# Four score blocks per exponential instead of two, and a layernorm that reads PSUM without a copy, in an eight-core transformer layer

## The chip, the cores and the metric

The kernel runs on the 8 cores of one Trainium2 chip, the same program on every core with other data. The metric is the device time of the slowest core in microseconds (us). Each core has a matrix engine (PE, with its weight loads shown apart as PEld), a vector engine (DVE), a scalar engine (ACT), GpSimd (POOL) and a queue engine (SP) that here only starts transfers. PE writes into PSUM, 2048 float32 columns in each of the two tensors `ps_a` and `ps_b2` of this kernel, cut into banks of 512 columns.

## The reference

Four sequences of 2048 tokens of width 2048 go through one attention layer and one gated MLP, each with a layernorm before and behind it:

```python
# attention: 16 query heads of 128, 4 key/value heads; causal, 1024 wide, plus the first 4 tokens
att = einsum('bkgqd,bkjd->bkgqj', q, k) / sqrt(128)
y   = softmax(where(mask, att, -inf)) @ v
# layer
x = x + layernorm(attention(layernorm(x)))            # _L0_attn_ref, Wq Wk Wv Wo
x = x + layernorm(ffn(layernorm(x)))                  # silu(h @ Wg.T) * (h @ Wu.T) @ Wd.T, 8192 wide
```

## The kernel before

Each core takes one half (1024 tokens) of one sequence as queries; keys and values cover up to 2048 tokens. Weights come in as float32 through two staging tiles (`stage`, L244) and are cast to bf16 on ACT or POOL. There is no scheduler: the Python code calls `em.task(engine, ...)`, each engine executes its tasks in the order of these calls, and the class `Em` works out from named tiles which semaphores a task waits for. A task waits only before its first instruction and signals only behind its last. So the order of the calls on each engine is the order of the work.

The stages, with times since the start of the span of the profiled execution:

- 0 to 367 us: layernorm of 16 token tiles, their transposes, and the k, v and q projections. The tile `xt` of 1 MB comes by a transfer that POOL issues (L354), K and V projections stand between (`kproj`, `vproj`).
- 367 to about 708 us: attention. A head is handled in two half-loops that run one head apart. `front_batch` (L436) makes scores: it multiplies one to two blocks of 128 keys with 512 queries into banks of `ps_a` (L448, 128x512 each), takes their exponential on ACT into `pt` in bf16 (L457) and multiplies by the mask on DVE (L476). The table `FRONT_B` gives the blocks of each batch; batches of even number use banks 0 and 1, those of odd number banks 2 and 3 (`base`, L440). `back_batch` (L487) handles the head before: four value matmuls and four matmuls with a column of ones (which sum the softmax) per batch of four blocks, by the table `BATCHES`, into `ps_b2`. `back_norm` (L521) belongs to the head before that: one matmul, then a copy, a logarithm and an exponential of 128x512 on ACT (L530, L532, L535), and a multiplication on DVE. The order within head `i` is: back batch 0 of head `i-1`, front batch 0, the norm of head `i-2`, front batch 1, back batch 1, front batches 2 and 3, and so on. There are 32 such heads: 16 over the first 512 queries (12 blocks of keys each, called the first half below), then 16 over the other 512 (13 blocks, the second half); between the halves another mask tile is loaded over the first.
- 708 to 862 us: output projection of 8 token tiles, layernorm, residual, second layernorm and transposes.
- 862 to 2200 us: the MLP in four quarters, PE after PE.
- 2200 to 2283 us, the last stage: for each of 8 token tiles, 16 float32 transposes (L769) bring the MLP's result from `out_fm` into PSUM, all of `ps_b2` for even tiles and all of `ps_a` for odd ones. ACT copies the tile to SBUF (L779), DVE takes its statistics (L785, L790). That is `e_stage1`. `e_stage2` makes the reciprocal deviation on ACT (L803, L806), the shift on DVE (L809), the normalised tile on ACT in place (L813), adds the residual on DVE (L819) and stores. The calls are `e_stage1(tb)`, then `e_stage2(tb - 1)` (L827 to L830).

Of the kernel before, what the change touches and what calls it, by code (L numbers as in the profile page):

```python
# [27 lines left out]
FRONT_B = [  # L28
    [(0, 2), (2, 2), (4, 2), (6, 2), (8, 2), (10, 2)],
    [(0, 2), (2, 2), (4, 2), (6, 2), (8, 2), (10, 2), (12, 1)],  # L30
]
# [95 lines left out]
def build_nc():  # L127
# [75 lines left out]
    pa = ps_a.ap()  # L203
# [145 lines left out]

    for idx, tb in enumerate(TB_ORDER):  # L350
# [3 lines left out]
        em.task("gpsimd",  # L354
                [lambda q, tb=tb, s=s: q.dma_start(out=xt[s].ap(),
                                                   in_=x_kv[tb * 128:(tb + 1) * 128, :])],
                writes=[f"xt{s}"], stream=f"xt{s}")
# [78 lines left out]
    def front_batch(qs, hh, bi):  # L436
        kl = KL[qs]
        kv = hh // 4
        st0, ln = FRONT_B[qs][bi]
        base = (bi % 2) * 2  # L440
        fns = []
        bkeys = []
        for j in range(ln):
            s_ = st0 + j
            kb = kl[s_]
            bkeys.append(PAK[base + j])
            fns.append(lambda t, kb=kb, kv=kv, dst=PA[base + j], qs=qs, hh=hh:
                       t.matmul(dst,  # L448
                                kf.ap()[:, kv * 2048 + kb * 128:kv * 2048 + (kb + 1) * 128],
                                qf.ap()[:, hh * 1024 + qs * 512:hh * 1024 + (qs + 1) * 512],  # L450
                                start=True, stop=True, skip_group_check=True))
# [5 lines left out]
                [lambda q, base=base, st0=st0, ln=ln: q.activation(  # L457
                    pt.ap()[:, st0 * 512:(st0 + ln) * 512],
                    pa[:, base * 512:(base + ln) * 512],
# [86 lines left out]
    for i, (qs, hh) in enumerate(HSEQ):  # L546
# [195 lines left out]
    def e_stage1(tb):  # L742
# [33 lines left out]
        war_o = [otkey + "ln"] + (["xo1"] if s == 1 else  # L776
                                  ["h2tok", "x2t_1", "x2p_1"])
# [16 lines left out]
    def e_stage2(tb):  # L794
# [6 lines left out]
        otkey = "outT" if s == 0 else "xo1"  # L801
        b6, b2_, rs, nm, _ = STT[par]
# [147 lines left out]
```

How the kernel before makes its waits and increments, by code:

```python
    def replay(self, eng_obj, eng_name, sems):  # L112
        for waits, fns, inc in self.items[eng_name]:
            for (s, v) in waits:
                eng_obj.wait_ge(sems[s], 16 * v if s in self.streams else v)
            last = None
            for fn in fns:
                last = fn(eng_obj)
            if inc is not None and last is not None:
                last.then_inc(sems[inc[0]], inc[1])
```

## Time and profile before

| | |
|---|---|
| median of 3 runs | 2284.46 us (2282.42 to 2285.09) |
| profiled execution | 2284.57 us; span of its slowest core, core 4: 2282.9 us |
| spans of the eight cores | 2269.5 to 2282.9 us, granted PE clock 0.969 to 0.972 on each |
| PE busy | 2025.4 us, 89% of the span |
| ACT busy | 955.6 us, 42% |
| DVE busy | 459.7 us, 20% |
| chain that ended last | PE 82%, ACT 9%, issue 4%, DVE 3%, DMA 2% |

Around the span lie 1.7 us of the profiled execution. A busy share is an average over stages of different kinds: what an edit is worth is read in its own stage, from which engine waits for which there. In the rows a matmul's end is modelled and neighbours overlap, so distances between starts are surer than lengths; a row with "x4" spans four instructions. A few matmul records are missing, so a row may say x1 where two instructions ran.

### The profile page before, as it was taken

Reading aid. Unit: us, or ns where it says so; the run is one execution under the profiler, and the core shown is the slowest. Engines: PE = TensorE matmul, PEld = TensorE weight load, DVE = VectorE, ACT = ScalarE, POOL = GpSimd, SP = SyncE. Lnnn points to the kernel's source line nnn. Section 1 sums busy time; section 2 is a strip of 40 time slices with the busy share of each in tenths; the row PEclk is TensorE's granted clock in tenths of the full one; section 3 lists DMA queues with packets and bytes.
Section 4 is the critical chain, followed back from the end, with each engine's and each line's share of the span. In section 5 each row is a group of like instructions: output and inputs, shape, how many; then the busy total and the mean of one; then the engine's idle time right before and its main releaser. Section 6 shows DMA issues by size and latency. Waiting matters only on the chain.

```text
span 2282.9 us, 24237 instructions; the slowest of 8 cores (2269.5 to 2282.9 us)
## 1 busy us (share of the span) xinstructions
PE 2025.4 (89%) x9241; PEld 897.6 (39%) x9424; DVE 459.7 (20%) x672; ACT 955.6 (42%) x1043; POOL 65.5 (3%) x87
## 2 busy tenths in 40 slices
PE   0677999998888878999999999999999999999971
PEld 0333443222223433444444444444444444444441
DVE  1122003553333450000110000110001110001134
ACT  3344346887774434333323333313333323333324
POOL 1100002400000000000000000000000000000000
PEclk9988999999999998999999999999999999999995
DMA  6321245501001334444643444534445534445515
GB/s 185 129 88 60 93 148 182 180 1 49 1 1 56 111 116 152 157 148 148 189 144 125 152 153 155 190 110 148 148 157 162 180 111 156 156 149 166 186 73 221
DMA packets 75570, 298.71 MB, mean 131 GB/s; under 512 B 8512, under 2 KB 8640, under 8 KB 69056
## 3 DMA queue, kind: packets, MB, share of 16 engines
q1 hardware_dynamic: 70848, 263.58, 35.8%
q0 software_dynamic: 4608, 33.56, 4.2%
q8 instruction: 77, 1.26, 0.2%
q14 instruction: 37, 0.30, 0.1%
HBM read 280.33 MB, written 16.78 MB: 130 GB/s over the span
## 4 chain that ended last, share of the span: by engine, by line
PE 82%; ACT 9%; issue 4%; DVE 3%; DMA 2%; ACTq 0%; DVEq 0%; SPq 0%; POOL 0%; POOLq 0%
PE ps_b L674 19%; PE ps_a L682 19%; PE ps_a L715 10%; PE ps_b L715 10%; PE ps_a L407 3%; PE ps_b L507 3%; PE ps_a L448 3%; ACT pt L457 3%; PE ps_b L498 3%; PE ps_a L590 3%; PE ps_b L590 2%; PE ps_a L312 2%; PE ps_a L327 2%; PE ps_b L407 2%; ACT h1t L375 1%
## 5 line engine op out<-in xcount | busy, mean ns | idle before, releaser
L253 ACT CAST wbf<-wst 128x1024 bf16<-128x1024 f32 x384 | 394.4, 1045 | 468.3 <-DMA wst<-wgu_pe 231.8
L674 PE MATMUL ps_b<-h2f,wbf 128*128 128x512 bf16 x2006 | 451.6, 380 | 6.5 <-ACT wbf L253 4.4
L682 PE MATMUL ps_a<-h2f,wbf 128*128 128x512 bf16 x2008 | 449.7, 379 | 2.1
L674 PEld LDWEIGHTS ps_b<-h2f,wbf 128*128 128x128 bf16 x2048 | 200.9, 98 | 247.3 <-issue 7.2
L682 PEld LDWEIGHTS ps_a<-h2f,wbf 128*128 128x128 bf16 x2048 | 200.4, 98 | 241.7
L694 DVE TENSOR_TENSOR a_sb<-silu_t,ps_a 128x1024 bf16<-128x1024 f32 x64 | 78.2, 1221 | 817.6 <-PE ps_a L682 578.4
L715 PE MATMUL ps_a<-a_sb,wbf 128*128 128x512 bf16 x1005 | 225.2, 379 | 6.9 <-DVE a_sb L694 5.9
L715 PE MATMUL ps_b<-a_sb,wbf 128*128 128x512 bf16 x1002 | 225.1, 379 | 1.2
L690 ACT ACTIVATE silu_t<-ps_b 128x1024 f32<-128x1024 f32 x64 | 65.6, 1025 | 380.4 <-PE ps_b L674 380.4
L457 ACT ACTIVATE pt<-ps_a 128x1024 bf16<-128x1024 f32 (+1 forms) x208 | 194.1, 987 | 69.6 <-PE ps_a L448 69.2
L476 DVE TENSOR_TENSOR pt<-pt,msk 128x1024 bf16<-128x1024 bf16 (+1 forms) x192 | 124.8, 662 | 292.2 <-ACT pt L457 283.0
L715 PEld LDWEIGHTS ps_a<-a_sb,wbf 128*128 128x128 bf16 x1024 | 99.9, 98 | 127.6 <-issue 7.8
L715 PEld LDWEIGHTS ps_b<-a_sb,wbf 128*128 128x128 bf16 x1024 | 100.2, 98 | 120.8
L448 PE MATMUL ps_a<-qf,kf 128*128 128x512 bf16 x387 | 113.7, 383 | 36.3 <-ACT pt L457 34.9
L383 PE MATMUL ps_b<-i,h1t 128*128 128x128 bf16 x256 | 23.2, 263 | 101.9 <-ACT h1t L375 101.9
L507 PE MATMUL ps_b<-pt,ones_bf 128*1 128x512 bf16 x400 | 105.2, 380 | 0.7
L498 PE MATMUL ps_b<-pt,vt 128*128 128x512 bf16 x388 | 102.6, 379 | 3.3 <-DVE pt L476 1.9
L407 PE MATMUL ps_a<-h1f,wqr 128*128 128x512 bf16 x344 | 76.5, 379 | 3.1 <-ACT wqr L253 2.7
L448 PEld LDWEIGHTS ps_a<-qf,kf 128*128 128x128 bf16 x400 | 26.6, 97 | 111.2 <-issue 103.2
L590 PE MATMUL ps_a<-wo_bf,yf 128*128 128x512 bf16 x249 | 57.6, 391 | 7.3 <-ACT h2f L636 4.6
L590 PE MATMUL ps_b<-wo_bf,yf 128*128 128x512 bf16 x252 | 57.3, 387 | 6.5 <-ACT h2f L636 6.3
L383 PEld LDWEIGHTS ps_b<-i,h1t 128*128 128x128 bf16 x256 | 20.0, 120 | 107.9 <-issue 107.9
(106 smaller groups left out, 1109.3 us busy)
## 6 DMA issues: line engine op xcount, KB each, us to landing
wst<-wgu_pe SPq DMA_DIRECT2D x256, 512.0 KB, 4.4
wst<-wd_pe SPq DMA_DIRECT2D x128, 512.0 KB, 4.5
xt<-x_kv POOLq DMA_DIRECT2D x16, 1024.0 KB, 5.2
wst<-wq_pe SPq DMA_DIRECT2D x32, 512.0 KB, 4.3
wst<-wo_t SPq DMA_DIRECT2D x32, 512.0 KB, 4.5
xo<-x_kv POOLq DMA_DIRECT2D x8, 1024.0 KB, 7.1
wst<-wk_pe SPq DMA_DIRECT2D x8, 512.0 KB, 4.7
wst<-wv_t SPq DMA_DIRECT2D x16, 256.0 KB, 3.9
```

The lines of the kernel that those rows point to most:

```text
L253: fn = [lambda g, d=dst_ap, sl=slot, n=n: g.copy(d, sl.ap()[:, 0:n])]
L407: fns.append(lambda t, r=r, ts=ts, c=c, bk=bk: t.matmul(bk, wqr[r].ap()[:, c * 128:(c + 1) * 128], h1f.ap()[:, c * 2048 + 1024 + ts * 512: ...
L448: t.matmul(dst, kf.ap()[:, kv * 2048 + kb * 128:kv * 2048 + (kb + 1) * 128], qf.ap()[:, hh * 1024 + qs * 512:hh * 1024 + (qs + 1) * 512], ...
L457: [lambda q, base=base, st0=st0, ln=ln: q.activation(pt.ap()[:, st0 * 512:(st0 + ln) * 512], pa[:, base * 512:(base + ln) * 512], AF.Exp, ...
L476: [lambda v, a=a, b=b: v.tensor_tensor(pt.ap()[:, a * 512:(a + b) * 512], pt.ap()[:, a * 512:(a + b) * 512], msk.ap()[:, a * 512:(a + b) * ...
L498: t.matmul(yb, vt.ap()[:, kb * 512 + kv * 128:kb * 512 + (kv + 1) * 128], pt.ap()[:, s_ * 512:(s_ + 1) * 512], start=first, stop=last, ski ...
L507: t.matmul(zb[0:1, :], ones_bf.ap(), pt.ap()[:, s_ * 512:(s_ + 1) * 512], start=first, stop=last, skip_group_check=True))
L590: fns.append(lambda t, c=c, ms=ms, tb=tb, bk=banks[ms][0]: t.matmul(bk, yf.ap()[:, c * 1024 + tb * 128:c * 1024 + (tb + 1) * 128], wo_bf.a ...
L674: fns.append(lambda t, c=c, ts=ts, rg=rg: t.matmul(PB[ts], wbf[rg].ap()[:, c * 128:(c + 1) * 128], h2f.ap()[:, c * 1024 + ts * 512:c * 102 ...
L682: fns.append(lambda t, c=c, ts=ts, ru=ru: t.matmul(pa[:, ts * 512:(ts + 1) * 512], wbf[ru].ap()[:, c * 128:(c + 1) * 128], h2f.ap()[:, c * ...
L694: [lambda v, jj=jj: v.tensor_tensor(a_sb.ap()[:, jj * 1024:(jj + 1) * 1024], silu_t.ap(), pa[:, 0:1024], ALU.mult)],
L715: fns.append(lambda t, ic=ic, ts=ts, r=r, dps=dps: t.matmul(dps[ts], wbf[r].ap()[:, ic * 128:(ic + 1) * 128], a_sb.ap()[:, ic * 1024 + ts ...
```

## The change

It has three parts.

1. In the attention stage the table `FRONT_B` goes; scores are made in the batches of `BATCHES`, four blocks at a time (and one block as a fourth batch in the second half), always from bank 0 of `ps_a` on. The exponential and the mask multiplication cover up to 128x2048 in one instruction. Back batch and front batch of the same number alternate.
2. In the last stage the copy from PSUM to SBUF goes. The statistics and the normalising activation read the transposed tile in PSUM.
3. In the first stage the call that issues the transfer of `xt` stands behind the calls of `vproj` and `kproj`.

```diff
-FRONT_B = [
-    [(0, 2), (2, 2), (4, 2), (6, 2), (8, 2), (10, 2)],
-    [(0, 2), (2, 2), (4, 2), (6, 2), (8, 2), (10, 2), (12, 1)],
-]
 BATCHES = [
     [(0, 4), (4, 4), (8, 4)],
     [(0, 4), (4, 4), (8, 4), (12, 1)],
 ...
     for idx, tb in enumerate(TB_ORDER):
-        em.task("gpsimd",
-                [lambda q, tb=tb, s=s: q.dma_start(out=xt[s].ap(),
-                                                   in_=x_kv[tb * 128:(tb + 1) * 128, :])],
-                writes=[f"xt{s}"], stream=f"xt{s}")
         if idx >= 6:
             while len(vback) > 1:
                 vproj(vback.pop(0))
 ...
             for m in range(4):
                 kproj(m, 0)
+        em.task("gpsimd",
+                [lambda q, tb=tb, s=s: q.dma_start(out=xt[s].ap(),
+                                                   in_=x_kv[tb * 128:(tb + 1) * 128, :])],
+                writes=[f"xt{s}"], stream=f"xt{s}")
 ...
     def front_batch(qs, hh, bi):
-        st0, ln = FRONT_B[qs][bi]
-        base = (bi % 2) * 2
+        st0, ln = BATCHES[qs][bi]
 ...
-            bkeys.append(PAK[base + j])
+            bkeys.append(PAK[j])
 ...
-                [lambda q, base=base, st0=st0, ln=ln: q.activation(
-                    pt.ap()[:, st0 * 512:(st0 + ln) * 512],
-                    pa[:, base * 512:(base + ln) * 512],
+                [lambda q, src=pa[:, 0:512 * ln], st0=st0, ln=ln: q.activation(
+                    pt.ap()[:, st0 * 512:(st0 + ln) * 512], src,
                     AF.Exp, scale=SCALE)],
 ...
-        for bi in range(nbf):
-            if bi % 2 == 0 and i >= 1 and bi // 2 < nbb:
-                back_batch(HSEQ[i - 1][0], HSEQ[i - 1][1], (i - 1) % 2, bi // 2)
-            front_batch(qs, hh, bi)
+        for bi in range(max(nbf, nbb)):
+            if i >= 1 and bi < nbb:
+                back_batch(HSEQ[i - 1][0], HSEQ[i - 1][1], (i - 1) % 2, bi)
+            if bi < nbf:
+                front_batch(qs, hh, bi)
             if bi == 0 and i >= 2:
                 back_norm(HSEQ[i - 2][0], HSEQ[i - 2][1], (i - 2) % 2)
 ...
-        em.task("scalar",
-                [lambda q, otbuf=otbuf, tsrc=tsrc: q.copy(otbuf.ap(), tsrc)],
-                reads=tkeys,
-                writes=[f"{otkey}_{g}" for g in range(4)], war=war_o)
         b6, b2_, rs, nm, _ = STT[par]
         fns = []
         for j in range(4):
-            fns.append(lambda v, j=j, b6=b6, otbuf=otbuf: v.bn_stats(
+            fns.append(lambda v, j=j, b6=b6, tsrc=tsrc: v.bn_stats(
                 b6.ap()[:, 6 * j:6 * j + 6],
-                otbuf.ap()[:, 512 * j:512 * (j + 1)]))
-        em.task("vector", fns, reads=[f"{otkey}_{g}" for g in range(4)],
-                writes=["bn6" + sx])
+                tsrc[:, 512 * j:512 * (j + 1)]))
+        em.task("vector", fns, reads=tkeys, writes=["bn6" + sx])
 ...
         em.task("scalar",
-                [lambda q, otbuf=otbuf, par=par: q.activation(
-                    otbuf.ap(), otbuf.ap(), AF.Identity,
+                [lambda q, otbuf=otbuf, par=par, tsrc=tsrc: q.activation(
+                    otbuf.ap(), tsrc, AF.Identity,
                     bias=STT[par][3].ap(), scale=STT[par][2].ap())],
-                reads=[f"{otkey}_{g}" for g in range(4)] + ["nmr" + sx, "rstd" + sx],
-                writes=[otkey + "ln"])
+                reads=tkeys + ["nmr" + sx, "rstd" + sx],
+                writes=[otkey + "ln"], war=war_o)
```

On PE, a head of the second half reads as follows before; `qf,kf` are score matmuls, `pt,vt` value matmuls, `pt,ones_bf` those with ones, and `zrow,ones_row` the one of the norm.

```order
L448 MATMUL ps_a<-qf,kf 128x512 x2
L526 MATMUL ps_b<-zrow_70,ones_row 128x512
L448 MATMUL ps_a<-qf,kf 128x512 x2
L498 MATMUL ps_b<-pt,vt 128x512 x4
L507 MATMUL ps_b<-pt,ones_bf 1x512 x4
L448 MATMUL ps_a<-qf,kf 128x512 x4
L498 MATMUL ps_b<-pt,vt 128x512 x4
L507 MATMUL ps_b<-pt,ones_bf 1x512 x4
L448 MATMUL ps_a<-qf,kf 128x512 x4
L498 MATMUL ps_b<-pt,vt 128x512
L507 MATMUL ps_b<-pt,ones_bf 1x512
L448 MATMUL ps_a<-qf,kf 128x512
```

With the change the same head reads:

```order
L442 MATMUL ps_a<-qf,kf 128x512 x4
L519 MATMUL ps_b<-zrow_70,ones_row 128x512
L491 MATMUL ps_b<-pt,vt 128x512 x4
L500 MATMUL ps_b<-pt,ones_bf 1x512 x4
L442 MATMUL ps_a<-qf,kf 128x512 x4
L491 MATMUL ps_b<-pt,vt 128x512 x4
L500 MATMUL ps_b<-pt,ones_bf 1x512 x4
L442 MATMUL ps_a<-qf,kf 128x512 x4
L491 MATMUL ps_b<-pt,vt 128x512
L500 MATMUL ps_b<-pt,ones_bf 1x512
L442 MATMUL ps_a<-qf,kf 128x512
```

The pairs of score matmuls became groups of four. The group that opens a head now stands whole ahead of the norm's matmul, and one group, not two pairs, stands between two back batches; the single last block still stands ahead of the next head's first back batch.

On ACT, the last stage begins like this before; `outT` and `xo_61` are the SBUF tiles, `ps_b` and `ps_a` the PSUM tensors of even and odd token tiles.

```order
L779 COPY outT<-ps_b 128x2048
L779 COPY xo_61<-ps_a 128x2048
L803 ACTIVATE rstd<-bn_85,eps_sb 128x1
L806 ACTIVATE rstd<-rstd 128x1
L813 ACTIVATE outT<-outT,nmr,rstd 128x2048
L779 COPY outT<-ps_b 128x2048
L803 ACTIVATE rstdb<-bn2b,eps_sb 128x1
L806 ACTIVATE rstdb<-rstdb 128x1
L813 ACTIVATE xo_61<-xo_61,nmrb,rstdb 128x2048
```

And with the change:

```order
L794 ACTIVATE rstd<-bn_85,eps_sb 128x1
L797 ACTIVATE rstd<-rstd 128x1
L806 ACTIVATE outT<-ps_b,nmr,rstd 128x2048
L794 ACTIVATE rstdb<-bn2b,eps_sb 128x1
L797 ACTIVATE rstdb<-rstdb 128x1
L806 ACTIVATE xo_61<-ps_a,nmrb,rstdb 128x2048
```

The copies are gone, and the activation that writes the normalised tile reads PSUM, in which the transposes of the tile after the next are to be put.

On DVE, late in the last stage, before:

```order
L785 BN_STATS bn_84<-outT 128x6 x4
L790 BN_AGGR bn_85<-bn_84 128x2
L809 TENSOR_SCALAR nmrb<-bn2b,rstdb 128x1
L819 TENSOR_TENSOR xo_60<-xo_60,xo_61 128x2048
L785 BN_STATS bn6b<-xo_61 128x6 x4
```

And with the change:

```order
L773 BN_STATS bn_84<-ps_b 128x6 x4
L777 BN_AGGR bn_85<-bn_84 128x2
L800 TENSOR_SCALAR nmrb<-bn2b,rstdb 128x1
L812 TENSOR_TENSOR xo_60<-xo_60,xo_61 128x2048
L773 BN_STATS bn6b<-ps_a 128x6 x4
```

The order is the same, and the statistics read PSUM.

On POOL and SP every instruction stands where it stood, with the same waits: between a call of `kproj` or `vproj` and the moved call nothing was issued on POOL. The part of PE's, ACT's and DVE's order that belongs to the first stage is the same too.

## Rows read from the trace of the kernel before

**Rows 1.** attention, by heads: us, PE, PEld, DVE, ACT, POOL busy (instructions), clock, DMA.
```profile
367.60:374.67 7.07, 5.12 (x21) 1.38 (x20) 4.51 (x6) 6.16 (x7) 3.07 (x3) 1.00 0.47 147
374.67:383.03 8.36, 8.36 (x38) 2.86 (x37) 4.13 (x6) 5.96 (x7) 3.13 (x3) 1.00 0.63 188
383.03:520.69 137.66, 124.08 (x508) 39.08 (x519) 73.25 (x100) 110.82 (x141) 32.10 (x26) 1.00 0.31 96
520.69:534.89 14.20, 10.55 (x39) 2.89 (x39) 4.15 (x8) 8.69 (x12) 0.00 (x0) 0.92 0.56 194
534.89:690.48 155.59, 136.51 (x549) 42.72 (x561) 55.38 (x98) 117.52 (x154) 0.00 (x0) 1.00 0.00 1
```

**Rows 2.** PE, second-half head: start us, us, instruction, [idle before <-releaser].
```profile
601.86 0.61 PE L448 MATMUL ps_a<-qf,kf 128*128 128x512 bf16 x2
...
603.16 1.03 PE L498 MATMUL ps_b<-pt,vt 128*128 128x512 bf16 x4
...
605.07 0.61 PE L448 MATMUL ps_a<-qf,kf 128*128 128x512 bf16 x2
...
608.90 1.04 PE L448 MATMUL ps_a<-qf,kf 128*128 128x512 bf16 x4
...
610.78 0.38 PE L448 MATMUL ps_a<-qf,kf 128*128 128x512 bf16 x1 [0.31 <-ACT pt L457]
```

**Rows 3.** ACT in the same head, same columns.
```profile
602.56 1.02 ACT L457 ACTIVATE pt<-ps_a 128x1024 bf16<-128x1024 f32 x1 [1.14 <-PE ps_a L448]
603.48 0.58 ACT L530 COPY zb_sb<-ps_b 128x512 f32<-128x512 f32 x1
...
605.41 2.86 ACT L457 ACTIVATE pt<-ps_a 128x1024 bf16<-128x1024 f32 x3
609.61 2.43 ACT L457 ACTIVATE pt<-ps_a 128x1024 bf16<-128x1024 f32 x3 [1.33 <-PE ps_a L448]
```

**Rows 4.** groups by shape, attention: busy us, mean ns | idle before us.
```profile
L457 ACT ACTIVATE pt<-ps_a 128x1024 bf16<-128x1024 f32 x192 | 186.3, 1019 | 69.6 <-PE ps_a L448 69.2 <-PE ps_b L507 0.4
...
L457 ACT ACTIVATE pt<-ps_a 128x512 bf16<-128x512 f32 x16 | 9.7, 604 | 0.0
```

**Rows 5.** the same columns, last stage.
```profile
L779 ACT COPY outT<-ps_b 128x2048 f32<-128x2048 f32 x4 | 7.5, 1867 | 40.4 <-PE ps_b L769 32.8 <-DVE x2t L819 7.7
```

**Rows 6.** the same columns, projection stage (inputs in PSUM).
```profile
L603 ACT ACTIVATE x2t<-ps_a,nmr,rstd 128x2048 f32<-128x2048 f32 x4 | 8.2, 2058 | 1.8 <-DVE nmr L294 1.8
```

**Rows 7.** PE as the first head begins, timeline.
```profile
368.61 0.59 PE L448 MATMUL ps_a<-qf,kf 128*128 128x512 bf16 x2 [0.39 <-ACT qf L414]
```

**Rows 8.** DVE and PE while the second masks load, timeline.
```profile
529.87 0.69 DVE L476 TENSOR_TENSOR pt<-pt,msk 128x1024 bf16<-128x1024 bf16 x1 [8.53 <-DMA msk<-masks]
...
531.91 1.25 PE L498 MATMUL ps_b<-pt,vt 128*128 128x512 bf16 x4 [1.93 <-DVE pt L476]
...
533.09 1.87 PE L507 MATMUL ps_b<-pt,ones_bf 128*1 128x512 bf16 x4
```

**Rows 9.** the last stage, timeline of all engines.
```profile
2203.42 1.91 PE L769 MATMUL ps_a<-i,out_fm 128*128 128x128 f32 x16
...
2205.70 2.47 DVE L785 BATCH_NORM_STATS2 bn<-outT 128x6 f32<-128x512 f32 x4 [3.33 <-ACT outT L779]
...
2218.00 2.47 DVE L785 BATCH_NORM_STATS2 bn<-outT 128x6 f32<-128x512 f32 x4 [2.06 <-ACT outT L779]
...
2227.60 2.47 DVE L785 BATCH_NORM_STATS2 bn6b<-xo 128x6 f32<-128x512 f32 x4 [2.06 <-ACT xo L779]
...
2227.65 3.65 PE L769 MATMUL ps_a<-i,out_fm 128*128 128x128 f32 x16 [5.96 <-ACT xo L779]
...
2230.36 0.15 DVE L809 TENSOR_SCALAR nmr<-bn,rstd 128x1 f32<-128x1 f32 x1
2230.60 2.09 ACT L813 ACTIVATE outT<-outT,nmr,rstd 128x2048 f32<-128x2048 f32 x1 [2.61 <-DVE nmr L809]
...
2266.39 2.47 DVE L785 BATCH_NORM_STATS2 bn6b<-xo 128x6 f32<-128x512 f32 x4 [2.06 <-ACT xo L779]
```

More of the change, by code:

```diff
@@ L445, in front_batch @@
             kb = kl[s_]
-            bkeys.append(PAK[base + j])
-            fns.append(lambda t, kb=kb, kv=kv, dst=PA[base + j], qs=qs, hh=hh:
+            bkeys.append(PAK[j])
+            fns.append(lambda t, kb=kb, kv=kv, dst=PA[j], qs=qs, hh=hh:
                        t.matmul(dst,
@@ L549, in build_nc @@
                     writes=["masks"], stream="msk")
-        nbf = len(FRONT_B[qs])
+        nbf = len(BATCHES[qs])
         nbb = len(BATCHES[HSEQ[i - 1][0]]) if i >= 1 else 0
-        for bi in range(nbf):
-            if bi % 2 == 0 and i >= 1 and bi // 2 < nbb:
-                back_batch(HSEQ[i - 1][0], HSEQ[i - 1][1], (i - 1) % 2, bi // 2)
-            front_batch(qs, hh, bi)
+        for bi in range(max(nbf, nbb)):
[3 more added lines that the diff above has]
+                front_batch(qs, hh, bi)
             if bi == 0 and i >= 2:
@@ L775, in e_stage1 @@
                     writes=[tppk])
-        war_o = [otkey + "ln"] + (["xo1"] if s == 1 else
-                                  ["h2tok", "x2t_1", "x2p_1"])
-        em.task("scalar",
-                [lambda q, otbuf=otbuf, tsrc=tsrc: q.copy(otbuf.ap(), tsrc)],
-                reads=tkeys,
-                writes=[f"{otkey}_{g}" for g in range(4)], war=war_o)
         b6, b2_, rs, nm, _ = STT[par]
@@ L801, in e_stage2 @@
         otkey = "outT" if s == 0 else "xo1"
+        if s == 0:
+            tsrc, tkeys = pb2, ["pB0", "pB1", "pC", "pZ"]
+        else:
+            tsrc, tkeys = pa, list(PAK)
         b6, b2_, rs, nm, _ = STT[par]
@@ L811, in e_stage2 @@
                 reads=["bn2" + sx, "rstd" + sx], writes=["nmr" + sx])
+        war_o = [otkey + "ln"] + (["xo1"] if s == 1 else
+                                  ["h2tok", "x2t_1", "x2p_1"])
         em.task("scalar",
-                [lambda q, otbuf=otbuf, par=par: q.activation(
-                    otbuf.ap(), otbuf.ap(), AF.Identity,
+                [lambda q, otbuf=otbuf, par=par, tsrc=tsrc: q.activation(
+                    otbuf.ap(), tsrc, AF.Identity,
                     bias=STT[par][3].ap(), scale=STT[par][2].ap())],
-                reads=[f"{otkey}_{g}" for g in range(4)] + ["nmr" + sx, "rstd" + sx],
-                writes=[otkey + "ln"])
+                reads=tkeys + ["nmr" + sx, "rstd" + sx],
+                writes=[otkey + "ln"], war=war_o)
         em.task("vector",
```

## The prediction

> **What bounds the kernel now.** I read the busy table and the chain of waits first: PE is busy 89% of the span and holds 82% of the chain, so outside stages where PE waits, nothing but PE's own work counts. Then I cut the span into stages and looked for those in which PE does wait. The change touches two of them: attention and the last stage. In both, a loop of several engines sets the pace.
>
> Attention. The heads are regular [rows 1]: 14 heads of the first half take 137.66 us, 9.83 each, and 14 of the second half 155.59 us, 11.11 each. One head shows the loop [rows 2, 3]. PE starts a pair of score matmuls at 601.86 and ACT its exponential at 602.56: 0.70 us. Exponentials in a row start (2.86 - 1.02)/2 = 0.92 apart. The norm's three ACT instructions hold ACT from 603.48 to 605.41: 1.93. An exponential that ends at 609.61 + 1.02 = 610.63 frees its two banks for a score matmul at 610.78: 0.15. Matmuls of 512 columns are (1.04 - 0.38)/3 = 0.22 apart, and a back batch of eight takes 605.07 - 603.16 = 1.91. A second-half head is then the chain: 0.70, exponential 0.92, norm 1.93, exponential 1.02, 0.15, two matmuls 0.44, back batch 1.91, 0.70, exponential 1.02, 0.15, single matmul 0.22, back batch 1.91, together 11.07, against 11.11 measured. Without the 0.15, 0.70 and 1.02 around the single block, and with four scores (0.88) in place, a first-half head is 0.70 + 0.92 + 1.93 + 1.02 + 0.15 + 0.44 + 1.91 + 0.88 + 1.91 = 9.86, against 9.83. The chain is understood to 0.05 us per head. What makes it short is that two banks are computed while ACT reads the other two.
>
> Last stage. Per tile 9.68 us, from (2266.39 - 2218.00)/5 [rows 9]: copy, statistics of this tile, shift and normalisation of the one before, residual add, and then the next copy, which waits for that add. PE's transposes lie beside it, in 3.65 us per tile.
>
> **The change, part by part.** The sum is made against the profiled execution, 2284.57 us, 0.1 above the median.
>
> The moved transfer: every POOL and SP instruction keeps its place and its waits, and so do the first stage's parts of the other queues. 0 us, with no cover needed; I see no bound other than 0.
>
> Attention. Now a batch fills all four banks, so the next scores wait for the whole exponential. What ACT takes for 128x2048 from PSUM in an exponential is not in the trace. From below: 604 ns at 512 and 1019 at 1024 [rows 4] give 415 per further 512, so 1.85. From above: two of 1.02, so 2.04. The copy of 128x2048 from PSUM took 1867 ns [rows 5]; it has the same shape and engine, and I take 1.87. That is hardly less than 0.92 + 1.02 = 1.94, so ACT wins 0.07 per batch. Followed by other ACT work it costs 1.87 - 0.10 = 1.77 (the overlap 1.02 - 0.92). From the start of four scores to the exponential: 0.70 + 2 x 0.22 = 1.14.
>
> First-half head: 1.14 + 1.77 + norm 1.93 + second exponential 1.87 + 0.15 + 1.14 + third 1.87 + 0.15 = 10.02. The back batches (1.91 each) lie beside exponentials and are no longer in the chain; PE has 3 x (1.91 + 0.88) + 0.3 = 8.7 of work in it. Against 9.83: +0.19, times 14 = +2.7.
>
> Second-half head: at 10.02 the single last block starts, because it too needs bank 0, which the third exponential holds. Then 0.22 for it, and 1.91 for the back batch that stands behind it on PE, before the next head's first scores: 12.15. The last exponential itself (604 ns) hides under that back batch. Against 11.11: +1.04, times 14 = +14.6. This is the main term: the 1.9 us back batch, which used to run while ACT worked off the other pair of banks, now comes after an idle stretch of PE of 12.15 - 9.4 (8.7 and the three extra matmuls) = 2.7 us per head.
>
> Special heads. The first has no back batches: three times 1.14 + 1.87 + 0.15 = 3.16, so 9.48, and its group of four also waits for the last cast of the q projection, on which only the second pair waited (368.61, not 367.60) [rows 7]: 1.0 + 9.5 - 7.07 [rows 1] = +3.4. The second has no norm: 9.48 - 8.36 = +1.1. In the head at the change of masks, PE waits for DVE, DVE for the mask transfer [rows 8], and that for the last mask multiplication of the first half, now over 2048 columns; twice 0.69 bounds it, so +0.0 to +1.3, I take +0.6. The last head ends with its single block: 10.02 against 610.78 - 601.86 = 8.92: +1.1. Sum of attention: 2.7 + 14.6 + 3.4 + 1.1 + 0.6 + 1.1 = +23.5.
>
> PE's clock in the first head: PE will work 0.88 of every 3.16 us. From 530.0 to 531.9 PE sat idle behind thin work and the granted clock fell to 1.2 GHz: a row of four matmuls then lasted 1.87 instead of 1.03 [rows 2, 8]. I expect that here, for some ten matmuls at 0.2 extra, less what the exponentials hide: +1.5, bounds 0 and +4.
>
> Last stage. Without the copy (1.87) tile 0's statistics start at 2205.70 - 1.9 = 2203.8 [rows 9], tile 1's 2.76 later (2227.60 to 2230.36, which spans statistics, aggregate and shift), tile 0's shift at 2209.3, its activation 0.24 later (2230.36 to 2230.60) for 2.06 from PSUM [rows 6]. Only then may PE overwrite that PSUM: the copy used to free it, and now the normalising activation does, a whole step later. Transposes at 2211.7, 3.65 long, statistics of tile 2 at 2215.5: 2.5 earlier than 2218.00. After that the loop is 2.76 + 0.24 + 2.06 + 0.15 + 3.65 + 0.15 = 9.01, since the transposes now stand in it and hide the residual add: -0.67, five times, -3.3. The end behind tile 7's statistics keeps its form. Total -5.8. So removing 1.87 us of ACT per tile gives back 0.67: late next are the transposes.
>
> Sum: 2284.57 + 23.5 + 1.5 - 5.8 = 2303.8, say 2304.
>
> **Rivals.** First, faster: the score matmuls are not held, and PE becomes the bound of attention. The place is the wait of each four-score group for the exponential before it; the price is PE's idle time, 15 x (9.83 - 8.7) + 15 x (11.11 - 9.4) = 43 us, which gives 2284.6 - 43 - 6 = 2236. It wins once the wait costs under 0.6 us a head in place of about 2. For it speaks that ACT waits 69 us for scores in this stage [rows 4] and fewer instructions go through it. Against it: all four banks are in one instruction, and the chain reproduces the present heads to 0.05 us with just this wait. The Trainium skill, Perfetto Trace Analysis, Optimizing Scalar/DVE Operations, says larger operations help throughput "if the engine is saturated", and that where ScalarE is not saturated but makes bubbles on other engines, smaller instructions may finish the work sooner. ACT is busy 117.52 of 155.59 us [rows 1], 76%, so by the second half of that rule the change has the wrong sign, as my sum says; by its first half alone it would gain 0.07 x 96 = 7 us and end at 2272. I give this rival 4 in 100.
>
> Second, slower still: PE's clock falls in each second-half head. By the chain above PE idles 1.0 us in such a head, does six matmuls, and idles 1.8. At the lower clock a back batch took 534.89 - 531.91 = 2.98 while the clock was falling [rows 1, 8], fully low 2 x 1.80 = 3.6, against 1.91: +1.7 in the chain, times 15 = +25, so 2329. For it: the fall at 531.9. Against it: there the wait alone was 1.93 us after nearly no work, and the present second half, PE 88% busy, keeps clock 1.00 [rows 1]. The Trainium skill, TensorE: Matmul & The Clock Gate, A second HAM failure mode, describes this for kernels that cycle through PSUM banks with micro-idles between groups; no row here shows it happening in a steady loop. 12 in 100; a third of it, 2312, lies in my range.
>
> Third: the single block hides after all, and a second-half head is as much longer as one of the first half. Then 14 x (1.04 - 0.19) = 12 less: 2292. PE's order speaks against it. 8 in 100.
>
> Fourth: with less idle between them the last transposes keep the full clock, 1.91 instead of 3.65 for 16 [rows 9]. Six tiles are 10 us less: 2293. Against it: PE's idle time between them stays above 5 us (9.01 - 3.65). 6 in 100.
>
> Fifth: the wide exponential takes 2.04. 96 of them, nearly all in the chain, are 16 us more: 2320. 6 in 100. That the change does nothing to the time would need the first and the other terms to cancel: no mechanism, part of the next line.
>
> **Numbers.** Forecast 64 in 100, with 2298 to 2310 as its own range. A measurement of this kernel tells about 0.2%, 4.6 us, from no change. Faster takes the first rival, 4 in 100; within 0.2% 4 in 100, for sums of the third and fourth; slower 92. The range reaches from below the third and fourth rival, 2290, to 2316, which takes in part of the second and fifth.
>
> **What would show it.** Second-half heads 12.1 us apart, first-half ones 10.0; exponentials of 128x2048 at 1.87; PE waiting twice a head about 1 us and nearly 2 us for ACT; two long ACT gaps of 1.3 us per head; no difference before 367 us and in the MLP; tiles of the last stage 9.0 apart with transposes directly behind the normalising activation. It would be wrong if second-half heads take under 11.5 us (third rival), if PE's clock is below 1.00 there (second), or if the last stage shrinks by over 10 us (fourth).

## The result, and the profile after

| | before | after |
|---|---|---|
| median of 10 runs each | 2284.23 us | 2323.73 us |
| lowest run | 2280.99 us | 2302.09 us |
| profiled execution | 2284.57 us | 2303.68 us |
| span of its slowest core | 2282.9 us (core 4) | 2302.1 us (core 2) |
| granted PE clock | 0.969 to 0.972 | 0.969 to 0.971 |
| PE, ACT, DVE busy | 2025.4, 955.6, 459.7 us | 2029.5, 935.2, 445.5 us |
| chain that ended last | PE 82%, ACT 9% | PE 78%, ACT 11% |

The time after is 1.0094 of the time before, with a 95% interval of 1.0081 to 1.0106: 21.5 us slower, for a forecast of 19.2 (2303.8 against 2284.57). The median of after lies above that because some of its runs were disturbed by a lower clock on one half of the chip or on both; the ratio leaves those out on both sides.

In the chain of the slowest core PE lost 4 points and ACT gained 2, though ACT is less busy than before. The forms of the exponential, grouped by shape (busy us, mean ns of one | idle us before them and who ended it), say where:

```profile
L451 ACT ACTIVATE pt<-ps_a 128x2048 bf16<-128x2048 f32 x96 | 179.7, 1871 | 89.7 <-PE ps_a L442 82.6 <-remote 7.1
...
L442 PE MATMUL ps_a<-qf,kf 128*128 128x512 bf16 x386 | 104.6, 384 | 61.0 <-ACT pt L451 59.4 <-ACT qf L409 0.8 <-PE ps_b L500 0.3
```

96 exponentials of 128x2048 took 1.87 us each, the value chosen from the copy of [rows 5]. The two halves of the price show in the idle times. PE waits 59.4 us for exponentials, where it waited 34.9 before:

```profile
L448 PE MATMUL ps_a<-qf,kf 128*128 128x512 bf16 x387 | 113.7, 383 | 36.3 <-ACT pt L457 34.9
```

ACT waits for scores 82.6 us ahead of the wide exponentials and 9.9 ahead of the single blocks', 92.5 in all, where it waited 69.2 [rows 4].

The windows of the attention stage, cut at the first score matmul of a head as in [rows 1], same columns: heads 1, 2, 3 to 16, 17, 18, and 19 to 31.

```profile
369.90:381.15 11.25, 6.79 (x19) 1.94 (x21) 3.36 (x3) 5.63 (x3) 4.52 (x5) 0.70 0.59 186
381.15:390.59 9.44, 8.54 (x37) 2.90 (x37) 3.90 (x4) 5.78 (x4) 3.92 (x3) 1.00 0.58 177
390.59:530.15 139.56, 123.44 (x508) 40.40 (x519) 63.31 (x57) 107.95 (x99) 28.68 (x24) 1.00 0.28 86
530.15:545.48 15.33, 11.04 (x39) 3.09 (x39) 4.54 (x6) 8.62 (x9) 0.00 (x0) 0.84 0.51 180
545.48:558.44 12.96, 10.32 (x40) 3.27 (x41) 3.73 (x5) 8.31 (x8) 0.00 (x0) 0.92 0.00 1
558.44:715.89 157.45, 124.97 (x510) 40.76 (x521) 48.43 (x65) 108.00 (x104) 0.00 (x0) 1.00 0.00 1
```

| heads | before [rows 1] | after | difference | forecast |
|---|---|---|---|---|
| 1 (without the later start) | 7.07 | 11.25 | +4.2 | +3.9 |
| 2 | 8.36 | 9.44 | +1.1 | +1.1 |
| 3 to 16 | 137.66 | 139.56 | +1.9 | +2.7 |
| 17 (change of masks) | 14.20 | 15.33 | +1.1 | +0.6 |
| 18 to 31 | 155.59 | 12.96 + 157.45 = 170.41 | +14.8 | +14.6 |
| 32, to its last score matmul | 8.9 | 10.0 | +1.1 | +1.1 |
| sum | | | +24.2 | +24.0 |

A head of the first half takes 139.56/14 = 9.97 (forecast 10.02), one of the second 157.45/13 = 12.11 (forecast 12.15). One of them on PE, as [rows 2] before:

```profile
594.81 1.04 PE L442 MATMUL ps_a<-qf,kf 128*128 128x512 bf16 x4
...
598.02 1.04 PE L442 MATMUL ps_a<-qf,kf 128*128 128x512 bf16 x4
...
601.65 1.02 PE L442 MATMUL ps_a<-qf,kf 128*128 128x512 bf16 x4 [0.78 <-ACT pt L451]
...
604.79 0.38 PE L442 MATMUL ps_a<-qf,kf 128*128 128x512 bf16 x1 [1.60 <-ACT pt L451]
...
605.00 1.02 PE L491 MATMUL ps_b<-pt,vt 128*128 128x512 bf16 x4
```

and on ACT, as [rows 3]:

```profile
595.94 1.88 ACT L451 ACTIVATE pt<-ps_a 128x2048 bf16<-128x2048 f32 x1 [1.78 <-PE ps_a L442]
...
597.72 0.58 ACT L523 COPY zb_sb<-ps_b 128x512 f32<-128x512 f32 x1
...
599.65 1.86 ACT L451 ACTIVATE pt<-ps_a 128x2048 bf16<-128x2048 f32 x1
...
602.77 1.88 ACT L451 ACTIVATE pt<-ps_a 128x2048 bf16<-128x2048 f32 x1 [1.26 <-PE ps_a L442]
```

This is the chain of the prediction, step by step. The exponential starts 1.13 behind the four scores (594.81 to 595.94), the norm 1.78 behind it, the second exponential 1.93 later; the scores that wait for it start at 601.65, 0.14 behind its end; the third exponential 1.12 later; and the single block at 604.79, 2.02 behind that. PE stands still 0.78 and 1.60 us, for "about 1" and "nearly 2" forecast; ACT waits 1.78 and 1.26 us, for two gaps of 1.3, since the back batch ahead of a head's first scores comes on top of the first. The back batch for which the next head's scores wait starts only at 605.00, behind the single block.

The first head, PE and ACT:

```profile
369.17 0.59 ACT L409 CAST qf<-ps_a 128x512 bf16<-128x512 f32 x1 [2.87 <-PE ps_a L402]
...
369.90 1.02 PE L442 MATMUL ps_a<-qf,kf 128*128 128x512 bf16 x4 [0.82 <-ACT qf L409]
...
373.04 1.50 PE L442 MATMUL ps_a<-qf,kf 128*128 128x512 bf16 x4 [2.12 <-ACT pt L451]
...
378.32 1.91 PE L491 MATMUL ps_b<-pt,vt 128*128 128x512 bf16 x4
```

The group of four waits for the last cast of the q projection, 0.73 behind its start, where the first pair used to start before it. Then PE works 1.0 of every 3.1 us, and the second group, four matmuls, spans 1.50 and the first value matmuls 1.91 in place of 1.04: the clock in this window is 0.70.

The change of masks, DVE and PE:

```profile
539.91 1.23 DVE L469 TENSOR_TENSOR pt<-pt,msk 128x2048 bf16<-128x2048 bf16 x1 [8.58 <-DMA msk<-masks]
...
541.88 1.86 PE L491 MATMUL ps_b<-pt,vt 128*128 128x512 bf16 x4 [1.39 <-DVE yf L533]
...
545.48 1.46 PE L442 MATMUL ps_a<-qf,kf 128*128 128x512 bf16 x3
```

PE's value matmuls wait, by the last event before them, for DVE's multiplication of `yf`, the norm's, which stands on DVE between the mask multiplication and the next one. From the head's first scores to the mask's arrival it is 9.76 us (530.15 to 539.91), against 529.87 - 520.69 = 9.18 [rows 1, 8]; PE restarts 1.97 behind it, against 2.04. Then all eight matmuls of the batch run at the level of 1.2 GHz, 3.60 us (541.88 to 545.48), against 2.98 in [rows 1, 8].

The last stage, statistics, activation and transposes, as [rows 9]:

```profile
2240.42 2.49 DVE L773 BATCH_NORM_STATS2 bn<-ps_b 128x6 f32<-128x512 f32 x4 [1.43 <-PE ps_b L763]
...
2249.39 2.49 DVE L773 BATCH_NORM_STATS2 bn6b<-ps_a 128x6 f32<-128x512 f32 x4 [1.43 <-PE ps_a L763]
...
2252.40 2.06 ACT L806 ACTIVATE outT<-ps_b,nmr,rstd 128x2048 f32<-128x2048 f32 x1 [6.43 <-DVE nmr L800]
...
2254.60 3.39 PE L763 MATMUL ps_b<-i,out_fm 128*128 128x128 f32 x16 [5.32 <-ACT outT L806]
...
2258.10 2.49 DVE L773 BATCH_NORM_STATS2 bn<-ps_b 128x6 f32<-128x512 f32 x4 [1.18 <-PE ps_b L763]
...
2285.00 2.49 DVE L773 BATCH_NORM_STATS2 bn6b<-ps_a 128x6 f32<-128x512 f32 x4 [1.44 <-PE ps_a L763]
```

Statistics start 8.97 apart (2240.42 to 2249.39), and 44.58/5 = 8.92 on average up to 2285.00, since one block of transposes was granted the full clock in part (3.39 in place of 3.65). The next transposes of a buffer start 0.14 behind the normalising activation, as foreseen, and statistics 3.50 behind those (3.75 behind the others, as 2245.64 to 2249.39, whose 16 transposes took 3.65). From the first transposes to the end of the last residual add it is 71.8 us, against 77.9 before: -6.1.

Between the last score matmul and the last stage the kernels are the same: 1501.4 us before, 1500.0 after. The spans differ by 19.2, and that is 24.2 for attention, -6.1 for the last stage, -1.5 for the MLP between them, +0.3 at the end and +2.3 at the start of attention. Of this last term 1.0 is the wait for the last cast; the rest is how far the slowest core's first stage ran late: over the eight cores the last cast starts between 361.8 and 367.9 before and between 363.3 and 369.2 after, with medians 0.2 apart. The three terms that no part of the change explains (-1.5, +0.3 and 1.3 of the +2.3) cancel to 0.1: that the two spans differ by just the forecast 19.2 is in part luck of these two executions, and over all runs it is 21.5.

### The profile page after: what moved, and what is told of

It is laid out like the page before. It is cut to its first block, busy times and chain, and to the rows that moved or that the text cites. A ratio compares the mean times of both kernels' runs of the same rounds, so it can differ in the third digit from the quotient of the medians.

```text
span 2302.1 us, 23791 instructions; the slowest of 8 cores (2294.8 to 2302.1 us)
## 1 busy us (share of the span) xinstructions
PE 2029.5 (88%) x9241; PEld 904.4 (39%) x9424; DVE 445.5 (19%) x592; ACT 935.2 (41%) x939; POOL 64.9 (3%) x87
## 3 DMA queue, kind: packets, MB, share of 16 engines
q8 instruction: 77, 1.26, 0.2%
## 4 chain that ended last, share of the span: by engine, by line
PE 78%; ACT 11%; issue 5%; DVE 2%; DMA 2%; another core or an unknown queue 0%; ACTq 0%; SPq 0%; DVEq 0%; POOL 0%; POOLq 0%
PE ps_b L668 19%; PE ps_a L676 19%; PE ps_a L709 10%; PE ps_b L709 10%; ACT pt L451 6%; PE ps_a L402 3%; PE ps_a L442 3%; PE ps_a L584 2%; PE ps_a L308 2%; PE ps_a L323 2%; PE ps_b L584 2%; PE ps_b L402 1%; ACT h1t L370 1%; PE ps_b L323 1%; DMA wst<-wk_pe 1%
## 5 line engine op out<-in xcount | busy, mean ns | idle before, releaser
L451 ACT ACTIVATE pt<-ps_a 128x2048 bf16<-128x2048 f32 x112 | 189.2, 1689 | 99.5 <-PE ps_a L442 92.5
L469 DVE TENSOR_TENSOR pt<-pt,msk 128x2048 bf16<-128x2048 bf16 (+1 forms) x112 | 110.4, 987 | 347.1 <-ACT pt L451 336.3
L442 PE MATMUL ps_a<-qf,kf 128*128 128x512 bf16 x386 | 104.6, 384 | 61.0 <-ACT pt L451 59.4
L442 PEld LDWEIGHTS ps_a<-qf,kf 128*128 128x128 bf16 x400 | 32.0, 97 | 132.2 <-issue 109.8
```

What stands on the lines that cost most here:

```text
L442: t.matmul(dst, kf.ap()[:, kv * 2048 + kb * 128:kv * 2048 + (kb + 1) * 128], qf.ap()[:, hh * 1024 + qs * 512:hh * 1024 + (qs + 1) * 512], ...
L451: [lambda q, src=pa[:, 0:512 * ln], st0=st0, ln=ln: q.activation(pt.ap()[:, st0 * 512:(st0 + ln) * 512], src, AF.Exp, scale=SCALE)],
L469: [lambda v, a=a, b=b: v.tensor_tensor(pt.ap()[:, a * 512:(a + b) * 512], pt.ap()[:, a * 512:(a + b) * 512], msk.ap()[:, a * 512:(a + b) * ...
```

## The experiments

Six kernels were run, and each ratio is to the kernel before on the same chip. The diffs are against the kernel named. The working theory is that of the prediction: in attention the price comes from an instruction that holds all four banks (and with them from PE's order behind a score group that waits), and the last stage pays with transposes what it saves in copies.

### Each part alone

First, the kernel before with part 2 only (the last stage of the kernel after):

> The kernel before with part 2 alone: the last stage reads PSUM without a copy. My theory: a tile of the last stage takes 9.0 us instead of 9.7, the stage 5.8 to 6.1 us less, so about 2278 us, ratio 0.9974. Rival (removing the copy gives nothing by itself, the whole difference of the two parts comes from attention): 2284, ratio 1.000. Rival (the copy's full 1.87 us per tile is gained when attention is as before): -15 us, 2269.

Measured: 0.9971 (0.9958 to 0.9984). Second, the kernel before with parts 1 and 3 (attention and the moved transfer):

> The kernel before with parts 1 and 3 alone: four score blocks per exponential, and the moved transfer. My theory: attention is 25 us longer (second-half heads 12.15 instead of 11.11 us, first-half heads 10.0 instead of 9.83, the first head 5 us), so about 2309 to 2311 us, ratio 1.011 to 1.012; this and e1 add up to the whole change, so the moved transfer is worth 0. Rival (parts interact or the moved transfer costs something): the sum of e1 and e2 misses the whole change by over 3 us.

Measured: 1.0117 (1.0095 to 1.0139), with heads 9.97 and 12.11 us apart. The two together make 1.0088, and the whole is 1.0094, which is inside the intervals: the parts add up, the last stage gives 0.3% and attention costs 1.2%. That says nothing of the moved transfer, which the second kernel contains, although the expectation drew it from the sum. Part 3 was not run alone. What speaks for 0 is that POOL runs the same 39 instructions in the same order in the first 360 us of core 0 before and after, and that the median start of the last cast over the cores moved by 0.2 us.

### The same order on PE, with instructions of two blocks

Is it the order (back batches and groups of four scores in turn) or the size of the instruction? Against the kernel after, PE's order stays as it is, and each group of four is two tasks, each with its own exponential and its own mask multiplication of 128x1024:

```diff
     def front_batch(qs, hh, bi):
-        st0, ln = BATCHES[qs][bi]
+        st, n = BATCHES[qs][bi]
+        for base in range(0, n, 2):
+            front_part(qs, hh, st + base, min(2, n - base), base)
+
+    def front_part(qs, hh, st0, ln, base):
...
-            bkeys.append(PAK[j])
+            bkeys.append(PAK[base + j])
...
-                [lambda q, src=pa[:, 0:512 * ln], st0=st0, ln=ln: q.activation(
+                [lambda q, src=pa[:, 512 * base:512 * (base + ln)], st0=st0, ln=ln: q.activation(
```

> The changed kernel, with its order of score groups and back batches on PE, but each group of four blocks is made by two tasks on each engine: scores into banks 0-1 and 2-3, an exponential of 128x1024 for each pair, a mask multiplication for each pair. My theory (the loss is that one instruction holds all four banks): the next pair of scores may start when the first exponential has ended, PE becomes the bound, a first-half head takes about 8.9 us and a second-half head about 9.9, attention is some 30 us under the kernel before and 55 under the changed one; with the last stage at -6 about 2248 us, ratio 0.984. Rival (the loss comes from the new order on PE, not from the width): no better than the changed kernel, ratio 1.009. Rival (only the fixed cost of the narrower instructions changes, 0.07 us per batch): 7 us slower than the changed kernel, ratio 1.012.

Measured: 0.9868 (0.9834 to 0.9902), 2.2% below the kernel after. Windows over 14 heads of the first half and 13 of the second, columns as above:

```profile
386.23:510.40 124.17, 124.17 (x520) 39.02 (x519) 75.03 (x98) 110.34 (x141) 27.14 (x25) 1.00 0.36 105
525.81:655.70 129.89, 127.03 (x522) 39.74 (x521) 51.41 (x91) 108.69 (x144) 0.00 (x0) 1.00 0.00 1
```

8.87 us per head in the first half, where PE is never seen idle, and 129.89/13 = 9.99 in the second. A head of the second half, PE and ACT in order of time:

```profile
563.25 1.04 PE L448 MATMUL ps_a<-qf,kf 128*128 128x512 bf16 x4
...
563.96 1.94 ACT L457 ACTIVATE pt<-ps_a 128x1024 bf16<-128x1024 f32 x2 [1.14 <-PE ps_a L448]
...
565.78 0.59 ACT L529 COPY zb_sb<-ps_b 128x512 f32<-128x512 f32 x1
...
566.46 1.04 PE L448 MATMUL ps_a<-qf,kf 128*128 128x512 bf16 x4
...
569.25 1.13 PE L448 MATMUL ps_a<-qf,kf 128*128 128x512 bf16 x4
...
569.95 2.43 ACT L457 ACTIVATE pt<-ps_a 128x1024 bf16<-128x1024 f32 x3 [0.31 <-PE ps_a L448]
...
571.12 0.38 PE L448 MATMUL ps_a<-qf,kf 128*128 128x512 bf16 x1 [0.22 <-ACT pt L457]
```

The scores of the next group are not waited for at all. The first pair of a group goes into banks that the first exponential has freed while the second exponential still reads the others, and the single block waits 0.22 in place of 1.60. By shape, its exponentials and score matmuls:

```profile
L457 ACT ACTIVATE pt<-ps_a 128x1024 bf16<-128x1024 f32 x192 | 185.4, 1018 | 41.5 <-PE ps_a L448 41.5
...
L448 PE MATMUL ps_a<-qf,kf 128*128 128x512 bf16 x400 | 108.8, 381 | 5.8 <-ACT pt L457 5.4 <-ACT qf L409 0.4
```

ACT does the same work with twice the instructions, 185.4 us against 179.7, and is idle before them for 41.5 us in place of 89.7; PE waits 5.4 us for them in place of 59.4. So order and size had opposite signs: the new order alone gains 1.3% with the shorter last stage (0.3% of it by the run above), and the wide instruction turns that into a loss.

What the new order is deserves a second look. Laid beside the kernel before, this kernel's attention differs in one thing only: the norm's instructions stand behind the head's second pair of scores and its exponential, no longer between the first pair and the second. Before, the norm's 1.93 us on ACT keep the second exponential waiting (602.56, norm at 603.48, the next at 605.41 [rows 3]), and with it the second pair of banks; here the two exponentials run in a row from 563.96 and the norm's copy follows at 565.78. PE's wait for exponentials goes from 34.9 us before to 5.4 by this alone.

Two things the run does not part. The wide form holds the banks longer, but it also starts later, 1.13 behind the first score in place of 0.71 (563.25 to 563.96), because it needs all four; both come from its size, and no run has one without the other. And the mask multiplication has half the width here too; it is hardly the cause, since PE's value matmuls wait 3.1 us in all in the kernel after and 4.7 here. The Trainium skill, Perfetto Trace Analysis, Optimizing Scalar/DVE Operations, says that smaller instructions may finish the work sooner where ScalarE is not saturated but makes bubbles elsewhere. The trace agrees: in the kernel after, ACT is busy 108.00 of the 157.45 us of heads 19 to 31, 69%, and the smaller instructions cost it 5.7 us and give PE back 54 us of waiting.

### The back batch ahead of the single block

The prediction put the second half's price on one place: the 1.9 us back batch behind a single block that waits. Against the kernel after, the first back batch of a head stands ahead of its own single last block:

```diff
-            if i >= 1 and bi < nbb:
+            if i >= 1 and bi < nbb and not (bi == 0 and HSEQ[i - 1][0] == 1):
                 back_batch(HSEQ[i - 1][0], HSEQ[i - 1][1], (i - 1) % 2, bi)
+            if bi == 3:
+                back_batch(qs, hh, i % 2, 0)
             if bi < nbf:
```

> The changed kernel, but in second-half heads the first back batch of the same head stands on PE ahead of the single thirteenth block, not behind it. My theory (the back batch of 1.91 us in the chain is the main term of the loss): it now lies beside the third exponential; the chain goes single block 0.22, to its exponential 0.48, exponential 0.60, 0.15, next scores, so a second-half head takes 10.02 + 0.49 + 0.60 + 0.15 = 11.3 us instead of 12.15, 15 heads 13 us less: about 2293 us, ratio 1.004. Rival (the long heads come from the third wide exponential or PE's clock, not from the back batch's place): a second-half head stays within 0.3 us of 12.15, ratio 1.008 to 1.010.

Measured: 1.0037 (1.0021 to 1.0052); heads of the second half 11.45 apart (first scores at 569.69, 581.15, 592.61), of the first 9.97 as in the kernel after. PE and ACT at the end of a head:

```profile
589.46 1.04 PE L491 MATMUL ps_b<-pt,vt 128*128 128x512 bf16 x4
...
591.38 0.39 PE L442 MATMUL ps_a<-qf,kf 128*128 128x512 bf16 x1
591.87 0.60 ACT L451 ACTIVATE pt<-ps_a 128x512 bf16<-128x512 f32 x1 [0.89 <-PE ps_a L442]
...
592.61 1.02 PE L442 MATMUL ps_a<-qf,kf 128*128 128x512 bf16 x4 [0.84 <-ACT pt L451]
```

The batch fills PE's wait, and the head is 0.66 shorter, for some 0.85 expected and not by the batch's whole 1.9: the single block now waits for the batch (it would have been free at 589.10 + 2.02 = 591.12 and starts at 591.38), and the next head's first scores need bank 0 too, which the single block's exponential holds for 0.84 more. The clock was 1.00 over heads 19 to 31, so it is no part of this. Heads 18 to 31 together are 8.9 us shorter than in the kernel after. The head at the change of masks is 1.7 longer (17.07 for 15.33): its single block now stands behind the batch that waits for the masks. The ratio fell by 0.0057, which is 13 us, and the spans differ by 12.2; what these heads leave of that lies outside them, and its cause is not shown. The place was right, and the rest of the price stays in the loop as long as each batch starts in bank 0.

### Batches of two throughout

Is the loop best cut in still finer steps? The kernel before, with back batches of two blocks, one ahead of each pair of scores:

```diff
-BATCHES = [
-    [(0, 4), (4, 4), (8, 4)],
-    [(0, 4), (4, 4), (8, 4), (12, 1)],
-]
+BATCHES = FRONT_B
...
-            if bi % 2 == 0 and i >= 1 and bi // 2 < nbb:
-                back_batch(HSEQ[i - 1][0], HSEQ[i - 1][1], (i - 1) % 2, bi // 2)
+            if i >= 1 and bi < nbb:
+                back_batch(HSEQ[i - 1][0], HSEQ[i - 1][1], (i - 1) % 2, bi)
             front_batch(qs, hh, bi)
```

> The kernel before with back batches of two blocks, one ahead of each pair of scores, instead of four blocks ahead of every second pair; exponentials of 128x1024 and the last stage as before. My theory (what matters is that an exponential never holds banks that the next scores need, and that no back batch of 1.9 us stands between an exponential's end and the next scores): PE bound, a head of the first half 8.9 to 9.3 us, one of the second 9.6 to 10.0, attention 25 to 30 us under the kernel before, so 2255 to 2260 us, ratio 0.988. Rival (groups of four back blocks are needed to cover an exponential): heads stay at 9.8 and 11.1, ratio 1.00.

Measured: 0.9949 (0.9933 to 0.9964), heads 9.66 and 10.23 apart: better than before, but by less than expected, and short of the two-block kernel even if the 0.3% of the last stage were added. PE in a first-half head:

```profile
426.90 0.60 PE L445 MATMUL ps_a<-qf,kf 128*128 128x512 bf16 x2
...
427.34 0.59 PE L495 MATMUL ps_b<-pt,vt 128*128 128x512 bf16 x2
...
427.86 0.59 PE L504 MATMUL ps_b<-pt,ones_bf 128*1 128x512 bf16 x2
...
428.39 0.61 PE L445 MATMUL ps_a<-qf,kf 128*128 128x512 bf16 x2
...
432.21 0.37 PE L523 MATMUL ps_b<-zrow,ones_row 1*128 1x512 bf16 x1 [0.23 <-ACT zrow L514]
```

A round of six matmuls takes 1.49 us (426.90 to 428.39), where half of a round of twelve (1.91 + 0.87) is 1.39. Two scores run into the value matmuls after 0.44, which is 2 x 0.22; these run into the ones after 0.52 and these into the next scores after 0.53, some 0.09 more than two matmuls each. In a round of twelve the same two changes are spread over twice the work. And the norm's matmul comes soon behind the sums that it needs and waits 0.23 for ACT. The direction was right, the size was not: PE bounds this kernel with a longer round. It waits only 1.3 us for exponentials although the norm stands where it stood before: finer batches remove that wait too, but the norm's place did it without the longer round.

### The last stage with four SBUF tiles

The other half of the change traded the copy for PSUM held longer. If instead the copy stays but goes to four SBUF tiles in turn (the two-block kernel, with the copy back and two more tiles), neither the residual add nor the activation holds anything that the transposes need:

```diff
+    ot2 = A("ot2", [128, 2048], F32, offset=65536)
+    ot3 = A("ot3", [128, 2048], F32, offset=73728)
...
-        otbuf = outT if s == 0 else xo[1]
+        otbuf = (outT, xo[1], ot2, ot3)[tb % 4]
```

> The kernel of e3 in attention; in the last stage the copy from PSUM to SBUF is back, into four SBUF tiles in turn instead of two (two new ones lie where the MLP's input was). My theory (not the copy's 1.87 us but its wait for the residual add of the tile before last set the pace of the kernel before, and in the changed one the late release of PSUM does): the copy of the next tile runs beside the add, transposes are off the chain, and a tile takes statistics to shift 2.76 + 0.24 + activation 2.09 + 0.18 + add 2.29 = 7.6 us, against 9.68 before and 9.0 in the changed kernel; the last stage is 6 us shorter than e3's, so about 2249 us, ratio 0.984. Rival (the stage is bound by its loads and stores of 2 MB per tile): tiles stay near 9 us, no gain over e3, ratio 0.987. Rival (the copy costs its own 1.87 us on ACT whatever waits for it): tiles of 9 to 9.7 us, e3 or slower.

Measured: 0.9871 (0.9850 to 0.9892), no better than the two-block kernel without it (0.9868). DVE's statistics and adds, with SP's issues of a store (L829) and of a load (L763), in order of time:

```profile
2181.86 2.47 DVE L787 BATCH_NORM_STATS2 bn<-ot 128x6 f32<-128x512 f32 x4
...
2189.33 2.46 DVE L787 BATCH_NORM_STATS2 bn6b<-ot 128x6 f32<-128x512 f32 x4
...
2194.57 2.29 DVE L825 TENSOR_TENSOR x2t<-x2t,ot 128x2048 f32<-128x2048 f32 x1 [2.36 <-ACT ot L819]
...
2197.06 0.36 SPq L829 DMA_DIRECT2D x_out<-x2t  x1
...
2205.76 0.32 SPq L763 DMA_DIRECT2D x2t<-x2s  x1
...
2212.49 2.29 DVE L825 TENSOR_TENSOR x2t<-x2t,outT 128x2048 f32<-128x2048 f32 x1 [4.24 <-DMA x2t<-x2s]
2214.70 2.46 DVE L787 BATCH_NORM_STATS2 bn<-ot 128x6 f32<-128x512 f32 x4
...
2223.93 2.46 DVE L787 BATCH_NORM_STATS2 bn6b<-ot 128x6 f32<-128x512 f32 x4
...
2231.35 2.29 DVE L825 TENSOR_TENSOR x2t<-x2t,ot 128x2048 f32<-128x2048 f32 x1 [4.53 <-DMA x2t<-x2s]
```

The theory held for the first tiles only: statistics 7.47 apart (2181.86 to 2189.33), against 8.97 in the kernel after. From 2205 on they are 9.2 to 9.3 apart (2214.70 to 2223.93), and the releaser of the add is a transfer: the add waits 4.2 to 4.5 us for its residual. The load of a residual goes into the tile out of which the result before the last is stored. The add of 2194.57 is stored at 2197.06, its load is issued 8.7 later at 2205.76, and the add that needs it starts 6.7 after that, at 2212.49: two tiles in 17.9, so 9.0 each and then 9.4. From the first transposes to the last add it is 75.8 us, where the two-block kernel has 71.6 and the kernel after 71.8: in its trace this stage is longer, by an amount (0.2%) that the ratios do not resolve. So behind the loop of engines stands one of transfers of about the same length. In it a store lands 7.9 to 8.6 us behind its issue and a load 6.4 to 6.7 (medians by tile), against 4.3 to 4.4 and 4.8 in the last stage of the kernel after, while the core moves about the same in 9 us, 232 to 235 GB/s against 231 to 262: loads and stores now lie over each other and each takes longer, which speaks for the transfers. More buffers for the residuals, which would tell whether the transfers themselves or the reuse of the tile sets these 9.0 us, were not tried.

## Why the prediction was right

Against its own steps:

- **The chain of a head.** 9.97 and 12.11 measured, 10.02 and 12.15 forecast. The 0.04 are in the overlap behind an exponential: the scores start 0.14, not 0.15, behind its end, four scores lead the exponential by 1.12 to 1.13, not 1.14, and one exponential in three took 1.86. That is -0.7 us over heads 3 to 16 (+1.9, not +2.7) and -0.5 over 19 to 31, where head 18 (12.96), whose first scores ran at the lower clock, gave 0.8 back: +14.8 for +14.6. That the banks held and what stands behind the wait on PE set it, and not the amount of work, is shown by two runs: with an exponential over two banks the wait is gone (9.99), and with the back batch ahead of the single block 0.66 of the 1.0 is.
- **The first head.** The later start was 1.0, as foreseen. The clock fell behind thin work as in [rows 8]: there PE had 0.38 us of work in the 3.13 us ahead of 531.91, after a stretch in which it was busy 7.20 of 8.09 us, and here 1.02 in the first 3.14. Head 1 took 11.25, which is 1.8 above the 9.48 of the chain, for 1.5 forecast; head 2 9.44 for 9.48.
- **The change of masks.** The term that was off by most for its size, +1.1 for +0.6, though inside its bounds of 0 and 1.3. The +0.6 put for the later transfer came (9.76 for 9.18). What had been left out is the back batch at the lower clock, 3.60 for 2.98, another +0.6, a cost that the second rival had named for another place.
- **The last head.** +1.1, as forecast.
- **The last stage.** -6.1 for -5.8: 8.92 per tile for 9.01, of which 0.05 are the one block of transposes that got part of the full clock. The total hides three smaller errors: the start gained 2.6 for 2.5, the five tiles of the loop 3.8 for 3.3, and the end, which was to keep its form, lost 0.3 (from tile 7's statistics to the last add 12.6 for 12.3). The run of this part alone gave 0.9971, 6.6 us, by itself.
- **The moved transfer.** Nothing that shows in the first stage; it was not run alone.

So the mechanism was right in both stages. The closeness of the sum owes something to luck: within attention -0.8 for heads 3 to 16 stands against +0.3 in the first head and +0.5 at the change of masks.

The rivals. That score matmuls would not be held is refuted by PE's 59.4 us of waiting, up from 34.9, and by the two-block run, in which they are not held and the time is 2.2% less: its sum, 2236, was nearer to that run (about 2254) than to the kernel. The clock fell in no steady head of the second half: 1.00 over 558.44 to 715.89. The Trainium skill, TensorE: Matmul & The Clock Gate, A second HAM failure mode, describes a fall for kernels that cycle through PSUM banks with short idles between groups; with idles of 0.78 and 1.60 us in each 12.11 it was not seen here, and in the first head, with idles of 2.12 behind 1.02 of work, the clock did fall. The single block did not hide (third rival): it is where PE waits 1.60. The last transposes kept 3.65 but for one (fourth), and the wide exponential took 1.87, not 2.04 (fifth).

## What to carry to other kernels

A wider instruction saves a fixed cost on its engine (here 0.07 us for two exponentials made one) and holds all its inputs until its end; where another engine refills those banks in the same loop, the hold can cost more than the saving, as it did here (PE's wait of 59.4 us against 5.4). So first write the loop of one round as a chain with the measured distances between starts, and see which wait the wider instruction moves and what stands behind it in its engine's order. Order and size are two changes: run them apart, since here the new order (in effect, the norm out from between two exponentials) gained and the new size lost more. And write out what a new order changes on each engine before giving it a name: here it was one move.

## What the runs showed beside this

- Going from value matmuls to those with ones, and from these to scores, costs PE some 0.09 us each; going from scores to value matmuls costs nothing that shows. So a back batch of eight takes 1.91 us where eight times 0.22 is 1.76, and finer rounds pay it more often.
- Batch statistics straight from PSUM took 2.49 us for 128x2048, from SBUF 2.47 [rows 9]; the normalising activation 2.06 from PSUM, 2.09 from SBUF [rows 9]. Where the data lies made no difference that counts in this stage; for how long it is held did.
- In the first head the clock was full (1.00) over 369.90 to 373.04 and fell to 1.2 GHz within the second group of scores (0.56 over 373.04 to 376.20), after 1.0 us of work and 2.12 of waiting; it was back at full by the ones matmuls at 380.16, and over the head it was 0.70.
